# Expert stage of a decoder layer: the down products of six of eight experts taken with the weights stationary and turned back on TensorE

## The chip, the core and the metric

The kernel runs on one core of one Trainium2 chip. The metric is the time of one execution on the device in microseconds (us), the median of several runs. A core has TensorE (PE in the rows, with its weight loads as PEld), VectorE (DVE), ScalarE (ACT), GpSimd (POOL), and a queue of transfers that SyncE issues (SP, SPq).

## What is computed

One decoder layer on 8 sequences of 112 tokens (896 tokens, width D = 512): causal self-attention, a linear cross-attention to a context, and a mixture of eight experts, each followed by a residual add and a layer norm. The change lies in the experts:

```
gate_up = einsum("th,ehj->etj", h, gate_up_proj) + gate_up_bias
gate, up = gate_up[..., ::2], gate_up[..., 1::2]
gate = minimum(gate, 7); up = clip(up, -7, 7)
act = (up + 1) * gate * sigmoid(1.702 * gate)
expert_out = einsum("eti,eih->eth", act, down_proj) + down_proj_bias
out = einsum("te,eth->th", scores, expert_out)      # two experts a token
```

## The kernel before

The program is written by hand, engine by engine; every instruction stands in a fixed queue and waits on counting semaphores. Each float32 matrix is held as a high and a low part (`_hi`, `_lo`), and `products` (L303) makes a product out of three matmuls for each of the KC = 4 chunks of 128 of the contraction, so 12 matmuls for one output bank.

Attention and routing end near 655 us. Routing has by then written each token's row into a table in DRAM (`x_rows`), with room for CAP = 288 rows an expert in a first round; later rounds exist in code and are entered only where an expert has more rows. The 288 rows are handled as PIECES of 128, 128 and 32 rows.

Expert e goes through these steps:

- **Gather.** `gather(e, k)` (L949) turns piece k of the expert's rows with four transposes into a bank (4 or 5 by `gather_bank`, L319); ScalarE (`gathered_high`, L1256) and VectorE (`gathered_low`, L1806) split it into `x_g`.
- **Gate/up.** `gate_up_part(e, q)` (L961), q = 0 to 3, makes 24 matmuls with 128 x 128 weights stationary and the 288 rows moving, into banks q % 2 and 2 + q % 2. Then VectorE clamps (`gl`, `up`), ScalarE takes the sigmoid (`sg`, `swish`), GpSimd multiplies (`pr`, `gated`), VectorE finishes (`hh`, `hidden`), and ScalarE and VectorE split that into `hT` (`h_high` L1269, `h_low`).
- **Down.** `down(e, k)` (L981), k = 0 to 2, has `hT` of a piece stationary (128, 128 and 32 columns) and the 512 columns of `w_dn` moving: 36 matmuls of 512 columns. The result of piece k has its rows on partitions, in bank 6, 7, and 4 or 5 (`y_bank`, L322).
- **Out.** ScalarE scales it by the routing score into `y` (`y_evac`, L1281), and GpSimd adds the rows into `y_acc` in DRAM by an indirect transfer (`add_rows`, L513). The adds of one expert wait until those of the expert before have landed.

TensorE's queue in iteration e (L995 to L1009) is: the four gate/up parts of e, with `gather(e + 1, q - 1)` behind part q = 1, 2 and 3; then the three down pieces of e - 1. The last iteration (e = 7) has no gathers, and `down(7)` follows `down(6)`. ScalarE's queue in iteration e (L1295 to L1320) has, for each q, a cast of the next expert's weights (`gu_high`), the sigmoid of part q, and the `hT` cast of part q - 1; at the end the `hT` cast of part 3, the two first `y_evac` of e - 1, the cast of the next down weights (`dn_high`), and the last `y_evac`. `splits_at` (L314) sets another order of the weight casts for experts 0 and 1: in iteration 1 three of them stand between the `hT` cast of part 3 and the first `y_evac`.

Two semaphores matter most here: `dn_mm` counts finished down pieces, and `y_out` counts `y_evac`. The first gather of an expert waits for the bank that a down result lay in:

```
if k == 0 and e >= 3:
    pe.wait_ge(m["y_out"], 3 * (e - 2))
```

which, for `gather(e + 1, 0)` in iteration e, asks for all three `y_evac` of expert e - 2. SyncE's queue (L424 to L433) loads the down weights of e + 1 once `dn_mm` has reached 3 * e, that is once expert e - 1 is finished with its own.

Of the kernel before, what the change touches and what calls it, by code (L numbers as in the profile page):

```python
# [12 lines left out]
P = 128  # L13
LN_EPS, DEN_EPS = 1e-5, 1e-6
ALPHA, LIMIT = 1.702, 7.0
CAP = 288
# [7 lines left out]
def decoder_layer(nc: bass.Bass, t: dict, out: bass.AP):  # L24
# [20 lines left out]
    with ExitStack() as ctx:  # L45
# [104 lines left out]
        def half_in(hf):  # L150
# [52 lines left out]
        hT = [r(f"hT{s}", 5888 + 2304 * s, (KC, CAP)) for s in range(2)]  # L203
        y = f("y", 24064, 4, D)
        gl = f("gl", 32112, 2, CAP)
        sg = f("sg", 32688, 2, CAP)
# [29 lines left out]
            ones_col sum_mm sum_out bn_ok mv_ok ve_ok rs_ok ln_ok t_hi q2_phi wx_hi wx_lo  # L236
            rz_ok ri_ok a_hi a_lo row_ok id_ok top_ok idx_ok topd_ok topf_ok hot_ok chosen_ok csum_ok dif_ok
            tw_ok prod_ok slotf_ok slot_ok sc_ok score_ok level_ok more_ok gub_ok gate_ok
            gu_hi gu_lo gu_mm gl_ok up_ok sg_ok pr_ok hh_ok h_hi h_lo dn_hi dn_lo dn_mm
            xg_mm xg_hi xg_lo y_out dnb_hi dnb_lo st_hi moreb_ok rest_ok""".split()  # L240
# [81 lines left out]
        def y_bank(e, k):  # L322
            return 6 + k if k < 2 else 4 + (e + 1) % 2
# [141 lines left out]
        def _(pool):  # L465
# [46 lines left out]

            def add_rows(c, number, slot):  # L513
                later = not isinstance(c, int)
                if later or c:
                    pool.wait_ge(add_done, 48 * c)
                    if later:
                        step()
                for k, (p0, rows) in enumerate(PIECES):
# [8 lines left out]
            for e in range(NE + 1):  # L528
                if e < NE:
                    for q in range(KC):  # L530
                        gated(e, q)
                if e == 1:
                    pool.wait_ge(base_out, 16 * (NT + 1))
                    pool.wait_ge(in_meta, 48)
                if e:
                    add_rows(e - 1, lambda k, rows: meta[0:rows, k, e - 1, NE:NE + 1], lambda k: (3 * (e - 1) + k) % 4)
            pool.wait_ge(m["more_ok"], 1)
# [16 lines left out]
        def _(pe):  # L554
# [421 lines left out]
            def down_piece(w, hid, k, bk):  # L976
                p0, rows = PIECES[k]
                products(banks[bk][0:rows, :], lambda a, i: hid[:, a, i, p0:p0 + rows],
                         lambda b, i: w[:, b, i, :], KC).then_inc(m["dn_mm"], 1)

            def down(e, k):  # L981
                if k == 0:
# [49 lines left out]
        def _(act):  # L1032
# [248 lines left out]
            def y_evac(e, k):  # L1281
# [13 lines left out]
            for e in range(NE):  # L1295
                more = e + 1 < NE
                for q in range(KC):
# [21 lines left out]
                if e:  # L1319
                    y_evac(e - 1, 2)  # L1320
            for k in range(3):
                y_evac(NE - 1, k)
            act.wait_ge(m["more_ok"], 1)
# [17 lines left out]
        def _(dve):  # L1341
# [201 lines left out]
            def choose(n):  # L1543
# [4 lines left out]
                dve.wait_ge(*done("rt", n))  # L1548
                nc.vector.max(top[:, s, :], logit[:, s, :]).then_inc(m["top_ok"], 1)
                dve.wait_ge(m["top_ok"], n + 1)  # L1550
                nc.vector.max_index(top_i[:, s, :], top[:, s, :], logit[:, s, :]).then_inc(m["idx_ok"], 1)
# [4 lines left out]
                dve.wait_ge(m["idx_ok"], n + 1)  # L1556
                nc.vector.tensor_copy(top_f[:, s, :], top_i[:, s, 0:2]).then_inc(m["topf_ok"], 1)
                dve.wait_ge(m["topf_ok"], n + 1)
                every = [P, 2, NE]
                nc.vector.tensor_tensor(hot[:, s], iota[:, :].unsqueeze(1).to_broadcast(every),  # L1560
                                        top_f[:, s, :].unsqueeze(2).to_broadcast(every), ALU.is_equal)\
                    .then_inc(m["hot_ok"], 1)
                dve.wait_ge(m["hot_ok"], n + 1)
                nc.vector.tensor_tensor(chosen[:, s, :], hot[:, s, 0], hot[:, s, 1], ALU.add)\
                    .then_inc(m["chosen_ok"], 1)
                nc.vector.tensor_tensor(dif[:, s, :], hot[:, s, 0], hot[:, s, 1], ALU.subtract)\
                    .then_inc(m["dif_ok"], 1)
                dve.wait_ge(m["chosen_ok"], n + 1)
# [4 lines left out]
            def assign(n):  # L1573
# [4 lines left out]
                dve.wait_ge(m["tw_ok"], n + 1)  # L1578
                dve.wait_ge(m["dif_ok"], n + 1)
                nc.vector.scalar_tensor_tensor(sc2[:, s, :], dif[:, s, :], tw[:, s:s + 1], chosen[:, s, :],  # L1580
                                               ALU.mult, ALU.add).then_inc(m["sc_ok"], 1)
                dve.wait_ge(*done("rk", n))
                nc.vector.tensor_tensor(prod[:, s], hot[:, s], pos[:, s, :].unsqueeze(1).to_broadcast([P, 2, NE]),
                                        ALU.mult).then_inc(m["prod_ok"], 1)
                dve.wait_ge(m["sc_ok"], n + 1)
                nc.vector.tensor_scalar(row[:, n, D:D + NE], sc2[:, s, :], 0.5, None, ALU.mult)\
                    .then_inc(m["score_ok"], 1)
                dve.wait_ge(m["prod_ok"], n + 1)
                nc.vector.tensor_reduce(slot_f[:, s, :], prod[:, s], AX.X, ALU.add).then_inc(m["slotf_ok"], 1)
                dve.wait_ge(m["slotf_ok"], n + 1)  # L1590
                nc.vector.tensor_copy(slot_u[:, n, :], slot_f[:, s, :]).then_inc(m["slot_ok"], 1)
# [369 lines left out]
```

## Time and profile before

| | |
|---|---|
| median of 3 runs | 872.35 us (871.97 to 874.51) |
| the profiled execution | 872.94 us, of which the span of the core is 871.1 us |
| TensorE busy | 828.2 us, 95% of the span |
| VectorE, ScalarE, GpSimd busy | 471.7, 310.4, 102.5 us |
| mean granted TensorE clock | 0.973 of full |

A row of the timeline gives start, duration, engine, line, operation, output<-inputs, shapes and count; in brackets stands the idle time before it and what ended that. The start of one group minus that of the one before is the time that the first took up; the durations of neighbours overlap by some 0.1 us. The granted clock (PEclk) is 1.00 at 2.4 GHz and 0.50 at 1.2 GHz.

### The profile page before, as it was taken

To read this page: it belongs to the slowest core of one execution; us is meant where nothing else is said; L and a number is where in the kernel's file an instruction comes from. 1 tells how busy PE (TensorE), PEld (TensorE's weight loads), DVE (VectorE), ACT (ScalarE), POOL (GpSimd) and SP (SyncE) were. 2 spreads that over 40 slices of the span, in tenths; PEclk is the share of its full clock that TensorE was granted. 3 is DMA by queue.
4 is the path that set the end of the run, shared out by engine and by line. 5 is a ranking of instruction groups with operands and counts; after the bars stand their busy time and mean duration, and the time that the engine had idled before them with its cause. 6 is when DMAs were issued, how large, how long until landed. Compare 5 with 4: busy or idle time off the path is not lost.

```text
span 871.1 us, 12501 instructions
## 1 busy us (share of the span) xinstructions
PE 828.2 (95%) x4878; PEld 728.1 (84%) x4878; DVE 471.7 (54%) x862; ACT 310.4 (36%) x700; POOL 102.5 (12%) x95
## 2 busy tenths in 40 slices
PE   7999999999999999999999999999988999999990
PEld 6989898989898898988899878888867888888860
DVE  4536455363635463575760244445686687777624
ACT  4443324242433432442443222221242465555430
POOL 0000000000000000000000000111131244434343
PEclk9999999999999999999999999999976999999995
DMA  9990724523020003003110100110376356656326
GB/s 330 334 295 6 226 109 167 163 81 121 9 94 6 26 6 121 3 4 133 50 36 1 35 6 35 57 61 9 123 284 196 134 190 199 199 173 173 76 34 192
DMA packets 35902, 97.91 MB, mean 112 GB/s; under 512 B 6648, under 2 KB 9080, under 8 KB 33152
## 3 DMA queue, kind: packets, MB, share of 16 engines
q1 hardware_dynamic: 32032, 88.62, 30.0%
q0 software_dynamic: 3808, 8.46, 4.9%
q8 instruction: 40, 0.66, 0.3%
q14 instruction: 22, 0.18, 0.1%
HBM read 64.03 MB, written 32.12 MB: 110 GB/s over the span
## 4 chain that ended last, share of the span: by engine, by line
PE 82%; DVE 7%; DMA 3%; issue 3%; ACT 3%; POOL 1%; POOLq 0%; SPq 0%; DVEq 0%
PE bank L306 66%; PE bank L667 3%; PE bank L701 3%; PE bank L596 3%; PE bank L760 2%; PE bank L655 1%; DVE w_gu L1343 1%; DVE prob L1390 1%; DMA raw_dn<-in_w_down_dram 1%; PE bank L945 1%; PE bank L573 1%; PE bank L739 1%; DMA y_acc<-y,meta 1%; ACT prob L1076 1%; DVE ln_st L1466 1%
## 5 line engine op out<-in xcount | busy, mean ns | idle before, releaser
L306 PE MATMUL bank<-w_kv,cT 128*125 128x512 f32 x576 | 143.6, 400 | 0.0
L306 PE MATMUL bank<-xT,w_qkv 128*128 128x512 f32 (+1 forms) x672 | 137.8, 365 | 0.2 <-ACT qT L1066 0.2
L306 PEld LDWEIGHTS bank<-xT,w_qkv 128*128 128x128 f32 x672 | 122.1, 188 | 15.2 <-ACT qT L1066 0.5
L306 PEld LDWEIGHTS bank<-w_kv,cT 128*125 128x125 f32 x576 | 104.2, 186 | 23.7
L306 PE MATMUL bank<-x_g,w_gu 128*128 128x288 f32 x768 | 111.7, 304 | 3.4 <-DVE x_g L1343 2.9
L306 PEld LDWEIGHTS bank<-x_g,w_gu 128*128 128x128 f32 x768 | 107.5, 195 | 5.1 <-issue 3.2
L475 POOL TENSOR_TENSOR ln_rs<-ln_ve,half 128x1 f32<-128x1 f32 (+2 forms) x16 | 12.7, 792 | 625.6 <-DVE ln_ve L1472 625.5
L306 PE MATMUL bank<-w_o,zT 128*128 128x512 f32 x336 | 79.8, 395 | 0.5 <-DVE acc L1678 0.5
L306 PE MATMUL bank<-w_qkv,xT 128*128 128x256 f32 x588 | 77.3, 287 | 0.0
L306 PEld LDWEIGHTS bank<-w_o,zT 128*128 128x128 f32 x336 | 61.7, 188 | 15.0 <-DVE acc L1377 1.8
L306 PEld LDWEIGHTS bank<-w_qkv,xT 128*128 128x128 f32 x588 | 72.2, 191 | 0.0
L306 PE MATMUL bank<-w_dn,hT 128*128 128x512 f32 (+1 forms) x288 | 68.4, 396 | 0.0
L306 PEld LDWEIGHTS bank<-w_dn,hT 128*128 128x128 f32 (+1 forms) x288 | 45.9, 161 | 19.3
L1343 DVE TENSOR_TENSOR w_qkv<-raw_w,w_qkv 128x1024 fp32r<-128x1024 f32 x21 | 25.7, 1225 | 61.2 <-ACT w_qkv L1034 61.2
L1076 ACT ACTIVATE prob<-prob,neg_max 112x112 f32<-112x112 f32 x128 | 47.7, 374 | 21.9 <-DVE neg_max L1394 21.9
L1103 ACT ACTIVATE relu_c<-bank 125x512 f32<-125x512 f32 x24 | 14.3, 598 | 111.1 <-PE bank L306 111.1
L1086 ACT CAST zT<-bank 128x448 fp32r<-128x448 f32 x32 | 17.0, 533 | 92.5 <-PE bank L667 92.5
L1343 DVE TENSOR_TENSOR w_gu<-raw_gu,w_gu 128x1024 fp32r<-128x1024 f32 x32 | 48.4, 1524 | 0.5 <-ACT w_gu L1034 0.5
L1377 DVE TENSOR_TENSOR acc<-acc,bank 128x512 f32<-128x512 f32 x49 | 33.6, 685 | 24.2 <-PE bank L306 24.2
L523 POOL DMA_INDIRECT y_acc<-y,meta x24 | 39.9, 1662 | 40.8 <-ACT y L1278 34.6
L506 POOL TENSOR_TENSOR pr<-gl,sg 128x288 f32<-128x288 f32 x32 | 32.6, 1019 | 88.3 <-ACT sg L1267 88.3
L1438 DVE SCALAR_TENSOR_TENSOR phi_k<-exp_c,relu_c 125x512 f32<-125x512 f32 x24 | 16.6, 692 | 48.2 <-ACT exp_c L1104 48.2
(150 smaller groups left out, 1155.3 us busy)
## 6 DMA issues: line engine op xcount, KB each, us to landing
x_rows<-blank SPq DMA_DIRECT2D x9, 2084.0 KB, 16.5
raw_gu<-in_w_gu_dram SPq DMA_DIRECT2D x8, 2048.0 KB, 7.8
raw_w<-in_w_qkv_dram SPq DMA_DIRECT2D x22, 512.0 KB, 8.1
raw_dn<-in_w_down_dram SPq DMA_DIRECT2D x8, 1024.0 KB, 9.1
raw_c<-in_ctx_t_dram SPq DMA_DIRECT2D x8, 750.0 KB, 4.3
raw_o<-in_w_o_dram SPq DMA_DIRECT2D x8, 512.0 KB, 4.1
xg<-x_rows SPq DMA_DIRECT2D x8, 512.0 KB, 5.6
raw_kv<-in_w_kv_dram SPq DMA_DIRECT2D x2, 1024.0 KB, 6.8
```

The lines of the kernel that those rows point to most:

```text
L306: last = nc.tensor.matmul(mm_out, lhs(a, k), rhs(b, k), start=(k == 0 and i == 0), stop=(k == n - 1 and i == 2))
L506: nc.gpsimd.tensor_tensor(pr[:, q % 2], gl[:, q % 2], sg[:, q % 2], ALU.mult)\
L523: nc.gpsimd.indirect_dma_start(y_acc, bass.IndirectOffsetOnAxis(ap=number(k, rows).bitcast(U32), axis=0), y[0:rows, slot(k), :], None, bou ...
L596: mm = nc.tensor.matmul(banks[j][:, half_in(hf)], w_first[:, part, a, k, h * E:(h + 1) * E], xT[:, b, k, half_of(hf)], start=(k == 0 and i ...
L667: mm = nc.tensor.matmul(banks[6 + g % 2][:, j * S:(j + 1) * S], V[0:S, p % 2, hf * BH + j, h * E:(h + 1) * E], probT[0:S, g % 2, j, :], st ...
L701: mm = nc.tensor.matmul(banks[4 + g // 2][:, (g % 2) * G1:(g % 2 + 1) * G1], phi_k[0:CM, n % 3, g * P:(g + 1) * P], v_c[0:CM, n % 3, g, :] ...
L760: mm = nc.tensor.matmul(bank("wo", n)[:, :], xT[:, a, k, n * P:(n + 1) * P], w_xo[:, b, k, :], start=(k == 0 and i == 0), stop=(k == KC - ...
L1076: e = nc.scalar.activation(prob[0:S, g, j, :], prob[0:S, g, j, :], ACT.Exp, bias=neg_max[0:S, i:i + 1], scale=-1.0, accum_out=exp_sum[0:S, ...
L1086: nc.scalar.copy(zT[:, 0, h, hf * HALF:(hf + 1) * HALF], banks[6 + g % 2][:, 0:HALF])\
L1343: return nc.vector.tensor_tensor(dst, src, bits(hi), ALU.subtract)
L1377: nc.vector.tensor_tensor(acc[:, n, :], acc[:, n, :], banks[n % 2][:, :], ALU.add)\
L1438: nc.vector.scalar_tensor_tensor(phi_k[0:CM, n % 3, :], exp_c[0:CM, n % 2, :], 1.0, relu_c[0:CM, n % 2, :], ALU.min, ALU.add).then_inc(m[" ...
```

## The change

For experts 0 to 5, `down_turned(e)` takes the place of `down(e, k)`. It has 128 x 128 blocks of `w_dn` stationary and the 288 columns of `hT` moving: four products of 12 matmuls, whose results (128 output columns on partitions, 288 rows along) lie alternately in banks 6 and 7. ScalarE copies each to the new tile `yT` (`y_turned`), and the third product waits for the first copy, the fourth for the second. One iteration later, behind gate/up part 0, `turn_y` turns `yT` back with 12 transposes against `ident` into the banks in which `down` had its results, and `dn_mm` now counts these. ScalarE's `y_evac` of that expert stands behind the sigmoid of part 0 (piece 0) and behind the sigmoid and the `hT` cast that follow part 1 (pieces 1 and 2). GpSimd's adds of expert e - 2 stand one each behind the multiply of parts 1, 2 and 3 of iteration e. Experts 6 and 7 keep `down`, both behind the last gate/up part. Some counters of VectorE's routing steps are merged into two (`pick_ok`, `put_ok`), with the same instructions in the same order.

```diff
+            def down_turned(e):
+                pe.wait_ge(m["dn_lo"], e + 1)
+                pe.wait_ge(m["h_lo"], KC * e + KC)
+                for j in range(KC):
+                    if j >= 2:
+                        pe.wait_ge(m["yt_ok"], KC * e + j - 1)
+                    elif e:
+                        pe.wait_ge(m["y_out"], 3 * (e - 1) + j + 1)
+                    products(banks[6 + j % 2][:, 0:CAP], lambda a, i: w_dn[e % 2][:, a, i, j * P:(j + 1) * P],
+                             lambda b, i: hT[e % 2][:, b, i, :], KC).then_inc(m["dt_mm"], 1)
+
+            def turn_y(e, k):
+                p0, rows = PIECES[k]
+                if k == 0:
+                    pe.wait_ge(m["yt_ok"], KC * e + KC)
+                if k == 2 and e + 2 < NE:
+                    pe.wait_ge(m["xg_lo"], 3 * (e + 2) + 3)
+                for j in range(KC):
+                    mm = nc.tensor.transpose(banks[y_bank(e, k)][0:rows, j * P:(j + 1) * P], yT[:, j, p0:p0 + rows],
+                                             ident[:, :])
+                mm.then_inc(m["dn_mm"], 1)
...
+                    if q == 0 and e >= 2:
+                        for k in range(3):
+                            turn_y(e - 2, k)
                 if e == 0:
                     for k in range(6, 8):
                         pe.wait_ge(free[k], LAST[k])
-                else:
-                    for k in range(3):
-                        down(e - 1, k)
-            for k in range(3):
-                down(NE - 1, k)
+                elif e + 1 < NE:
+                    down_turned(e - 1)
+            for e in (NE - 2, NE - 1):
+                for k in range(3):
+                    down(e, k)
...
+            def y_turned(e):
+                for j in range(KC):
+                    act.wait_ge(m["dt_mm"], KC * e + j + 1)
+                    if j == 0 and e:
+                        act.wait_ge(m["dn_mm"], 3 * e)
+                    nc.scalar.copy(yT[:, j, :], banks[6 + j % 2][:, 0:CAP]).then_inc(m["yt_ok"], 1)
...
+                    if q == 0 and e >= 2:
+                        y_evac(e - 2, 0)
+                    if q == 1 and e >= 2:
+                        y_evac(e - 2, 1)
+                        y_evac(e - 2, 2)
...
-                if e:
-                    y_evac(e - 1, 0)
-                    y_evac(e - 1, 1)
+                if e and more:
+                    y_turned(e - 1)
                 if more:
                     dn_high(e, e % 2)
-                if e:
-                    y_evac(e - 1, 2)
```

How the queues stand before and after, in iteration 5 or 6. Line numbers of the changed file differ by a few (L306, L945, L1273, L1278, L1267, L1034 are now L307, L951, L1304, L1309, L1298, L1065).

TensorE before, from gate/up part 0 of an expert (two runs of 24 `x_g,w_gu` matmuls are parts 0 and 1) to the first gather of the next:

```order
L306 MATMUL bank<-x_g_113,w_gu_101 128x288 [waits up_ok,xg_lo,gu_lo]
L306 MATMUL bank<-x_g_113,w_gu_101 128x288 x23
L306 MATMUL bank<-x_g_113,w_gu_101 128x288 [waits up_ok]
L306 MATMUL bank<-x_g_113,w_gu_101 128x288 x23
L945 MATMUL bank<-ident,xg_110 128x128 [waits y_out,xg_lo,in_xg1]
L945 MATMUL bank<-ident,xg_110 128x128 x3
```

TensorE with the change, from the third product of `down_turned` to the same gather:

```order
L307 MATMUL bank<-hT_115,w_dn_105 128x288 [waits yt_ok]
L307 MATMUL bank<-hT_115,w_dn_105 128x288 x11
L307 MATMUL bank<-hT_115,w_dn_105 128x288 [waits yt_ok]
L307 MATMUL bank<-hT_115,w_dn_105 128x288 x11
L307 MATMUL bank<-x_g_113,w_gu_101 128x288 [waits up_ok,xg_lo,gu_lo]
L307 MATMUL bank<-x_g_113,w_gu_101 128x288 x23
L1005 MATMUL bank<-ident,yT 128x128 [waits yt_ok]
L1005 MATMUL bank<-ident,yT 128x128 x7
...
L307 MATMUL bank<-x_g_113,w_gu_101 128x288 [waits up_ok]
L307 MATMUL bank<-x_g_113,w_gu_101 128x288 x23
L951 MATMUL bank<-ident,xg_110 128x128 [waits y_out,xg_lo,in_xg1]
```

The gather's wait on `y_out` is as it was and asks for the same three `y_evac`; two waits on `yt_ok` are new in the down products.

ScalarE before, from the last gather cast of an iteration through parts 0 and 1 of the next:

```order
L1259 CAST x_g_113<-bank 128x4x32 [waits xg_mm]
L1273 CAST hT_116<-hh 128x288 [waits dn_mm,hh_ok]
L1278 ACTIVATE y<-bank,meta 128x512 [waits dn_mm,add_done] x2
L1034 CAST w_dn_106<-raw_dn_108 128x2048 [waits in_dn1]
L1278 ACTIVATE y<-bank,meta 32x512 [waits dn_mm,add_done]
L1034 CAST w_gu_102<-raw_gu_104 128x1024 [waits in_gu1]
L1267 ACTIVATE sg<-gl 128x288 [waits pr_ok,gl_ok]
L1034 CAST w_gu_102<-raw_gu_104 128x1024 [waits in_gu1]
L1267 ACTIVATE sg<-gl 128x288 [waits pr_ok,gl_ok]
L1273 CAST hT_115<-hh 128x288 [waits dn_mm,hh_ok]
```

ScalarE with the change, the same stretch:

```order
L1304 CAST hT_116<-hh 128x288 [waits dn_mm,hh_ok]
L1326 COPY yT<-bank 128x288 [waits dn_mm,dt_mm]
L1326 COPY yT<-bank 128x288 [waits dt_mm] x3
L1065 CAST w_dn_106<-raw_dn_108 128x2048 [waits in_dn1]
L1065 CAST w_gu_102<-raw_gu_104 128x1024 [waits in_gu1]
L1298 ACTIVATE sg<-gl 128x288 [waits pr_ok,gl_ok]
L1309 ACTIVATE y<-bank,meta 128x512 [waits dn_mm,add_done]
L1065 CAST w_gu_102<-raw_gu_104 128x1024 [waits in_gu1]
L1298 ACTIVATE sg<-gl 128x288 [waits pr_ok,gl_ok]
L1304 CAST hT_115<-hh 128x288 [waits dn_mm,hh_ok]
L1309 ACTIVATE y<-bank,meta 128x512 [waits dn_mm,add_done]
L1309 ACTIVATE y<-bank,meta 32x512 [waits dn_mm,add_done]
```

The four copies of `yT` stand behind the `hT` cast of part 3, and the last two scalings into `y` behind the sigmoid of part 1.

## Rows read from the trace of the kernel before

**Rows 1.** The page, part 1: busy time of each engine.

```profile
PE 828.2 (95%) x4878; PEld 728.1 (84%) x4878; DVE 471.7 (54%) x862; ACT 310.4 (36%) x700; POOL 102.5 (12%) x95
```

**Rows 2.** Timeline of TensorE, iteration of expert 4, in order of time.

```profile
750.00 6.55 PE L306 MATMUL bank<-x_g,w_gu 128*128 128x288 f32 x48
756.39 0.60 PE L945 MATMUL bank<-ident,xg 128*128 128x128 f32 x4
756.75 3.44 PE L306 MATMUL bank<-x_g,w_gu 128*128 128x288 f32 x24
760.03 0.60 PE L945 MATMUL bank<-ident,xg 128*128 128x128 f32 x4
...
764.30 8.59 PE L306 MATMUL bank<-w_dn,hT 128*128 128x512 f32 x36
772.73 6.55 PE L306 MATMUL bank<-x_g,w_gu 128*128 128x288 f32 x48
```

**Rows 3.** Timeline of ScalarE, same iteration: behind part 1, and behind part 3.

```profile
757.94 0.43 ACT L1273 CAST hT<-hh 128x288 fp32r<-128x288 f32 x1 [0.34 <-DVE hh L1836]
758.27 1.05 ACT L1034 CAST w_gu<-raw_gu 128x1024 fp32r<-128x1024 f32 x1
...
768.59 0.43 ACT L1273 CAST hT<-hh 128x288 fp32r<-128x288 f32 x1 [2.00 <-DVE hh L1836]
768.93 0.68 ACT L1278 ACTIVATE y<-bank,meta 128x512 f32<-128x512 f32 x1
```

**Rows 4.** Timeline of ScalarE, end of iteration 1.

```profile
699.80 2.94 ACT L1034 CAST w_gu<-raw_gu 128x1024 fp32r<-128x1024 f32 x3
702.65 1.26 ACT L1278 ACTIVATE y<-bank,meta 128x512 f32<-128x512 f32 x2
```

**Rows 5.** Timeline of TensorE, end of iteration 1 and start of 2.

```profile
695.29 8.61 PE L306 MATMUL bank<-w_dn,hT 128*128 128x512 f32 x36
704.43 6.66 PE L306 MATMUL bank<-x_g,w_gu 128*128 128x288 f32 x48 [0.53 <-DVE w_gu L1343]
```

**Rows 6.** Windows: length, busy time (instructions) by engine, granted clock, DMA share, GB/s.

```profile
660.70:666.60 5.90, 5.86 (x24) 5.89 (x25) 4.49 (x5) 1.44 (x2) 0.00 (x0) 0.50 0.94 316
678.00:679.58 1.58, 0.00 (x0) 0.03 (x1) 1.34 (x4) 0.60 (x2) 0.66 (x1) 1.00 0.83 166
679.58:680.30 0.72, 0.72 (x5) 0.72 (x6) 0.45 (x1) 0.24 (x1) 0.13 (x1) 1.00 0.42 137
680.30:683.70 3.40, 3.40 (x17) 3.40 (x16) 1.33 (x4) 2.43 (x3) 0.00 (x0) 0.50 0.98 419
704.00:706.00 2.00, 1.57 (x12) 1.57 (x13) 0.65 (x2) 2.00 (x2) 1.62 (x1) 1.00 0.55 82
750.00:772.73 22.73, 22.61 (x146) 19.81 (x145) 16.78 (x24) 12.19 (x19) 9.27 (x8) 1.00 0.64 191
```

**Rows 7.** Timeline of TensorE and SyncE's queue, start of iteration 7.

```profile
818.19 12.95 PE L306 MATMUL bank<-x_g,w_gu 128*128 128x288 f32 x96
...
818.39 0.33 SPq L433 DMA_DIRECT2D raw_dn<-in_w_down_dram  x1
```

**Rows 8.** Chain of work that ended last, from iteration 7: start, duration, what.

```profile
818.39 8.50 DMA raw_dn<-in_w_down_dram
826.91 1.91 ACT w_dn L1034
...
841.54 3.77 DMA y_acc<-y,meta
```

**Rows 9.** Timeline of GpSimd, from the multiply of part 3 of iteration 7.

```profile
834.32 0.90 POOL L506 TENSOR_TENSOR pr<-gl,sg 128x288 f32<-128x288 f32 x1 [1.30 <-ACT sg L1267]
837.80 1.58 POOL L523 DMA_INDIRECT y_acc<-y,meta  x1 [2.58 <-ACT y L1278]
...
849.78 1.34 POOL L523 DMA_INDIRECT y_acc<-y,meta  x1 [0.31 <-issue]
```

**Rows 10.** Groups by line and form, 600 to 871: busy us, mean ns of one, idle before.

```profile
L945 PE MATMUL bank<-ident,xg 128*128 128x128 f32 x64 | 10.3, 291 | 2.5 <-DMA xg<-x_rows 2.5
```

More of the change, by code:

```diff
@@ L204, in decoder_layer @@
         y = f("y", 24064, 4, D)
+        yT = f("yT", 30208, KC, CAP)
         gl = f("gl", 32112, 2, CAP)
@@ L511, in step, with add_rows @@
                 pool.drain()
-            def add_rows(c, number, slot):
+            def add_rows(c, number, slot, which=(0, 1, 2)):
                 later = not isinstance(c, int)
-                if later or c:
+                if (later or c) and which[0] == 0:
                     pool.wait_ge(add_done, 48 * c)
@@ L518, in add_rows @@
                         step()
-                for k, (p0, rows) in enumerate(PIECES):
+                for k in which:
+                    p0, rows = PIECES[k]
                     pool.wait_ge(m["y_out"], 3 * c + k + 1)
@@ L526, in add_rows, with add_tiled @@
                         .then_inc(add_done, 16)
[L528 to L534, printed above, removed]
-                if e:
-                    add_rows(e - 1, lambda k, rows: meta[0:rows, k, e - 1, NE:NE + 1], lambda k: (3 * (e - 1) + k) % 4)
+            def add_tiled(e, which):
+                add_rows(e, lambda k, rows: meta[0:rows, k, e, NE:NE + 1], lambda k: (3 * e + k) % 4, which)
+            for e in range(NE):
+                for q in range(KC):
+                    gated(e, q)
+                    if e == 2 and q == 1:
+                        pool.wait_ge(base_out, 16 * (NT + 1))
+                        pool.wait_ge(in_meta, 48)
+                    if q and e >= 2:
+                        add_tiled(e - 2, (q - 1,))
+            for e in (NE - 2, NE - 1):
+                add_tiled(e, (0, 1, 2))
             pool.wait_ge(m["more_ok"], 1)
@@ L979, in down_piece @@
                          lambda b, i: w[:, b, i, :], KC).then_inc(m["dn_mm"], 1)
+            def down_turned(e):
[9 more added lines that the diff above has]
+            def turn_y(e, k):
+                p0, rows = PIECES[k]
+                if k == 0:
[6 more added lines that the diff above has]
+                mm.then_inc(m["dn_mm"], 1)
             def down(e, k):
@@ L1006, in _ @@
                         pe.wait_ge(free[k], LAST[k])
-                else:
-                    for k in range(3):
-                        down(e - 1, k)
-            for k in range(3):
-                down(NE - 1, k)
+                elif e + 1 < NE:
+                    down_turned(e - 1)
+            for e in (NE - 2, NE - 1):
+                for k in range(3):
+                    down(e, k)
             pe.wait_ge(m["more_ok"], 1)
@@ L1313, in _ @@
                     gu_high(e + 1, (e + 1) % 2, k)
-                if e:
-                    y_evac(e - 1, 0)
-                    y_evac(e - 1, 1)
+                if e and more:
+                    y_turned(e - 1)
                 if more:
                     dn_high(e, e % 2)
-                if e:
-                    y_evac(e - 1, 2)
-            for k in range(3):
-                y_evac(NE - 1, k)
+            for e in (NE - 2, NE - 1):
+                for k in range(3):
+                    y_evac(e, k)
             act.wait_ge(m["more_ok"], 1)
@@ L1548, in choose @@
                 dve.wait_ge(*done("rt", n))
-                nc.vector.max(top[:, s, :], logit[:, s, :]).then_inc(m["top_ok"], 1)
-                dve.wait_ge(m["top_ok"], n + 1)
-                nc.vector.max_index(top_i[:, s, :], top[:, s, :], logit[:, s, :]).then_inc(m["idx_ok"], 1)
+                nc.vector.max(top[:, s, :], logit[:, s, :]).then_inc(m["pick_ok"], 1)
+                dve.wait_ge(m["pick_ok"], 5 * n + 1)
+                nc.vector.max_index(top_i[:, s, :], top[:, s, :], logit[:, s, :]).then_inc(m["pick_ok"], 1)
                 if n >= 2:
@@ L1555, in choose @@
                     .then_inc(m["topd_ok"], 1)
[L1556 to L1558 removed]
+                dve.wait_ge(m["pick_ok"], 5 * n + 2)
+                nc.vector.tensor_copy(top_f[:, s, :], top_i[:, s, 0:2]).then_inc(m["pick_ok"], 1)
+                dve.wait_ge(m["pick_ok"], 5 * n + 3)
                 every = [P, 2, NE]
@@ L1578, in assign @@
                 dve.wait_ge(m["tw_ok"], n + 1)
-                dve.wait_ge(m["dif_ok"], n + 1)
+                dve.wait_ge(m["pick_ok"], 5 * n + 5)
                 nc.vector.scalar_tensor_tensor(sc2[:, s, :], dif[:, s, :], tw[:, s:s + 1], chosen[:, s, :],
-                                               ALU.mult, ALU.add).then_inc(m["sc_ok"], 1)
+                                               ALU.mult, ALU.add).then_inc(m["put_ok"], 1)
                 dve.wait_ge(*done("rk", n))
                 nc.vector.tensor_tensor(prod[:, s], hot[:, s], pos[:, s, :].unsqueeze(1).to_broadcast([P, 2, NE]),
-                                        ALU.mult).then_inc(m["prod_ok"], 1)
-                dve.wait_ge(m["sc_ok"], n + 1)
+                                        ALU.mult).then_inc(m["put_ok"], 1)
+                dve.wait_ge(m["put_ok"], 3 * n + 1)
                 nc.vector.tensor_scalar(row[:, n, D:D + NE], sc2[:, s, :], 0.5, None, ALU.mult)\
                     .then_inc(m["score_ok"], 1)
-                dve.wait_ge(m["prod_ok"], n + 1)
-                nc.vector.tensor_reduce(slot_f[:, s, :], prod[:, s], AX.X, ALU.add).then_inc(m["slotf_ok"], 1)
-                dve.wait_ge(m["slotf_ok"], n + 1)
+                dve.wait_ge(m["put_ok"], 3 * n + 2)
+                nc.vector.tensor_reduce(slot_f[:, s, :], prod[:, s], AX.X, ALU.add).then_inc(m["put_ok"], 1)
+                dve.wait_ge(m["put_ok"], 3 * n + 3)
                 nc.vector.tensor_copy(slot_u[:, n, :], slot_f[:, s, :]).then_inc(m["slot_ok"], 1)
```

12 lines of the change are left out of this document (6 added, 6 removed).

## The prediction

> **What bounds the kernel now.** I read the busy times first: TensorE is busy 828.2 of 871.1 us [rows 1], so TensorE's queue is the bound and the other engines count only where TensorE waits for them. The windows confirm it for the changed stage: in the iteration of expert 4, from 750.00 to 772.73, TensorE is busy 22.61 of 22.73 us at a clock of 1.00, VectorE 16.78 and ScalarE 12.19 [rows 6]. Next I read TensorE's timeline for that iteration [rows 2], since starts of neighbouring groups give real costs: 48 gate/up matmuls with 288 columns moving take 756.39 - 750.00 = 6.39 us, four transposes take 756.75 - 756.39 = 0.36, the 36 down matmuls take 772.73 - 764.30 = 8.43. Then ScalarE's timeline [rows 3, 4], because the change hangs TensorE on ScalarE in two places; last the end of the program [rows 7 to 9], which is a chain of transfers and adds and no longer TensorE alone. The sum is made against the profiled execution, 872.94 us; the median of the runs is 0.6 lower. About 0.3%, 2.6 us, is what a measurement of this kernel can tell from no change.
>
> **TensorE's work.** Per turned expert the change removes 36 matmuls of 512 columns, 8.43 us, and adds 48 of 288 columns. The same shape with the same count stands in the gate/up parts: 6.39 us [rows 2]. It adds 12 transposes; I take those of the gather, 0.36 us for four, so 1.08 [rows 2]. Net 8.43 - 6.39 - 1.08 = **0.96 us less**, times six 5.8. That is the whole gain, if nothing waits.
>
> The Trainium skill, TensorE: Matmul & The Clock Gate, section "Part 4: PE-mode transpose", puts a 128x128 transpose at about 275 ns in a kernel's context, and with it the turn-back would cost an estimated 3.3 us an expert. The gather rows say 90 ns for the same form, and the measurement decides.
>
> **New wait 1: the gather.** `gather(e + 1, 0)` stands right behind gate/up part 1 and needs all three `y_evac` of e - 2. Before, these were a whole iteration old. Now the last two stand on ScalarE behind the sigmoid of part 1 and the `hT` cast behind it, so they cannot begin before part 1 has ended and gone through VectorE and ScalarE. The trace shows this path already: part 1 ends at 756.39 [rows 2], that `hT` cast runs at 757.94 and ScalarE is free for the next instruction at 758.27 [rows 3]. Two scalings into `y` take 1.26 us [rows 4], so the gather may start at 759.53, **3.14 us late**. It happens in iterations 2 to 6, five times. Behind it in the queue stand parts 2 and 3, the other gathers and the next down products, and nothing can pass.
>
> **New wait 2: the third down product.** Products 0 and 1 need 24 x 288-column matmuls, 3.20 us (half of 6.39). Product 2 needs copy 0 out of bank 6, and that copy stands on ScalarE behind the `hT` cast of part 3. The down stretch begins at 764.30 [rows 2]; ScalarE begins its first instruction behind that cast at 768.93 [rows 3], the copy is of the cast's size, 0.43, say 0.45 with its signal: 769.38, against 767.50 when TensorE gets there: **1.88 us late**. The `hT` cast is that late since VectorE has a weight split and gather splits ahead of the last `hh`; none of that moves. Product 3 finds its copy done. This happens in iterations 2 to 6, five times. In iteration 1 three weight casts stand between: ScalarE is free at 702.65 [rows 4], the copy ends at 703.10, and TensorE, which began the down stretch at 695.29 [rows 5], waits from 698.49, **4.61 us**. Gate/up of expert 2 then begins at 703.10 + 3.20 = 706.30 in place of 704.43: 1.87 us later in all.
>
> **Sum for the iterations.** For 2 to 6: 22.73 - 8.43 + 6.39 + 1.08 + 3.14 + 1.88 = 26.79, which is 4.06 more; times five 20.3. With iteration 1: **22.2 us**.
>
> **What I cost at nothing.** ScalarE gets four copies of 0.45 us, 1.8 on 12.19 busy of 22.73 [rows 6]. The cast of the down weights now stands behind the last copy, so VectorE's low part of them ends a little into the next iteration and delays the clamps of part 0 by about a microsecond; part 2 needs those only 4 us later. SyncE loads the next down weights after the turn-back, 4.4 us into the next iteration in place of its start; the transfer takes 8.5 us [rows 8] and its cast is wanted at the end of that iteration, 20 us in. Row loads queued behind it are wanted an iteration later. GpSimd's adds go between its multiplies, 1.6 us each in gaps of 3 us. The merged counters have the same instructions in the same order on one engine.
>
> **The end.** In iteration 7 this cover is gone. The load of expert 7's down weights is issued 0.20 us after the start of gate/up [rows 7], and its cast holds up ScalarE's queue at part 1 [rows 8]. Now it is issued behind gate/up part 0 (3.28 us, rows 2: 756.75 to 760.03) and the turn-back (1.08): 4.36 us later, and the multiply of part 3, at 834.32 - 818.19 = 16.13 us into the iteration [rows 9], comes at 20.49. On GpSimd the last add of expert 5 now stands behind it: 0.90 for the multiply, then 3.77 until the add has landed [rows 8], 25.16. Only then may the adds of expert 6 start, which began at 837.80 - 818.19 = 19.61 [rows 9]: **5.6 us later**. From there to the last add it is 12.0 us as before, on the same chain of adds.
>
> Waits and work together: 22.2 + 5.6 = **27.8 us**.
>
> **The clock.** The only comparable wait in the stage shows what a pause does. TensorE idles from 678.00 to 679.58, goes on at 1.00 for 0.72 us, is granted 0.50 (1.2 GHz) from 680.30 to 683.70 and has 1.00 (2.4 GHz) in the windows from 704.00 on [rows 6]. In those 3.40 us it does half the work: 1.70 us lost. The pause of 0.53 us before 704.43 [rows 5] cost nothing, the clock stayed at 1.00 [rows 6]. All eleven new pauses (five of 3.14, five of 1.88, one of 4.61) are longer than the one of 1.58. Their price is bounded below by nothing (the fall might not come every time) and above by the stretch from 660.70 to 666.60, 5.90 us at 0.50 after a pause that came on top of little work [rows 6], 2.95 us. I take the nearest row, 1.70: 11 x 1.70 = **18.7 us**. Nothing hides it, since it falls on TensorE's own work.
>
> The forecast is 872.94 + 27.8 + 18.7 = 919.4, less 0.6 to the median: **919 us**.
>
> **Rivals.**
>
> 1. *The clock stays up.* One fall is little evidence, and between the new pauses TensorE always has at least 3 us of dense work. If none came: 872.35 + 27.8 = 900 us. Against it: the shorter pause did bring one. If only the six long ones did, 910. I give the whole of "no fall" 0.07; the part case belongs to the forecast.
>
> 2. *Falls or turns cost more than taken.* With 2.95 us a pause: 872.35 + 27.8 + 32.5 = 933 us. A mechanism of the same size is the turn-back itself, if its transposes, whose stationary operand ScalarE has just written, do not stream as the gather's do: at the gather transposes' own duration, 291 ns from start to end [rows 10], twelve take 3.5 us in place of 1.08, and 919 + 6 x 2.4 = 933. Against both: these transposes have the gather's form, and in this iteration four of them cost 0.36 us [rows 2]. Chance 0.06 for the clock, 0.03 for the transposes. The page's 275 ns stands for the same case and would give 932 by its estimate.
>
> 3. *Faster: the results are out in time.* ScalarE has 10.5 us free in an iteration, and TensorE is the bound; if `y_evac` of e - 2 and copy 0 came before TensorE asks, only the 0.96 us an expert would be left: 872.35 - 5.8 = 867 us, if the later load at the end were hidden too. The place is the first gather of iterations 2 to 6, and it decides by whether that gather starts less than 0.96 us after part 1 has ended. Against it: the scalings stand behind a sigmoid that part 1 itself feeds; 1.9 us pass in rows 2 and 3 before ScalarE is free even without them. 0.03.
>
> 4. *The waits are half as long*, because work that a late TensorE lets the others finish shortens the chains: about 872.35 + 5.6 + 1.9 + 5 x 1.5 + 11 x 0.85 = 897 us. Against it: both chains start at the end of a gate/up part, so lateness elsewhere does not shorten them. 0.04.
>
> **How the numbers follow.** Forecast 0.77, rivals 0.07, 0.09, 0.03, 0.04. The range runs from 902, a little above no falls, to 931, a little below the dear cases; at most 2 in 10 lie outside. Faster by over 0.3%: 0.03. Within 0.3%: 0.02, room for rival 3 if the end stays as late. Slower: 0.95.
>
> **What would show it.** In the changed profile: TensorE's first gather of iterations 2 to 6 with some 3.1 us idle before it, ended by ACT `y`; the 288-column down matmuls with 1.9 us idle in their middle, ended by ACT `yT`, 4.6 in the first expert; 12 transposes in 1.1 us; starts of gate/up 26.8 us apart plus up to 3.4 for the clock; 0.50 in windows behind each pause; the load of the last down weights 4.4 us into iteration 7. I would be wrong if the gather started at once, if the clock were 1.00 in windows behind the pauses, or if iterations were shorter than 22.7 us.

## The result, and the profile after

The changed kernel takes 906.27 us (902.9 to 908.92, 4 runs) against 873.43 us (4 runs) of the kernel before: a ratio of 1.037, 95% interval 1.034 to 1.041, so 3.7% slower. The forecast was 919 with a range of 902 to 931. The profiled execution took 902.9 us, 30.0 more than the one of before. Below, a fall means that the granted clock went from 1.00 to 0.50 for some microseconds, and gate/up 2 means the gate/up parts of expert 2.

TensorE's timeline in the iteration of expert 3, which answers to [rows 2]: start, duration, work, and in brackets the idle time before it with what ended it.

```profile
733.68 3.36 PE L307 MATMUL bank<-x_g,w_gu 128*128 128x288 f32 x24
736.88 1.47 PE L1005 MATMUL bank<-ident,yT 128*128 128x128 f32 x12
738.11 3.44 PE L307 MATMUL bank<-x_g,w_gu 128*128 128x288 f32 x24
744.65 0.63 PE L951 MATMUL bank<-ident,xg 128*128 128x128 f32 x4 [3.10 <-ACT y L1309]
745.04 3.43 PE L307 MATMUL bank<-x_g,w_gu 128*128 128x288 f32 x24
...
752.58 3.46 PE L307 MATMUL bank<-hT,w_dn 128*128 128x288 f32 x24
757.65 3.46 PE L307 MATMUL bank<-hT,w_dn 128*128 128x288 f32 x24 [1.61 <-ACT yT L1326]
760.95 3.36 PE L307 MATMUL bank<-x_g,w_gu 128*128 128x288 f32 x24
```

Both pauses are where the forecast put them, ended by the instructions it named. The iteration takes 760.95 - 733.68 = 27.27 us in place of 22.73, and the same 27.27 in each of the five. The waits of TensorE over the whole stage (total, times, longest):

```profile
PE bank L951 <- ACT y L1309: 15.5, 5, 3.1
PE bank L307 <- ACT yT L1326: 12.4, 6, 4.3
```

ScalarE's timeline at the two places answers to [rows 3]:

```profile
742.14 0.44 ACT L1298 ACTIVATE sg<-gl 128x288 f32<-128x288 f32 x1 [1.30 <-DVE gl L1864]
742.93 0.43 ACT L1304 CAST hT<-hh 128x288 fp32r<-128x288 f32 x1 [0.34 <-DVE hh L1877]
743.26 1.24 ACT L1309 ACTIVATE y<-bank,meta 128x512 f32<-128x512 f32 x2
...
756.87 0.43 ACT L1304 CAST hT<-hh 128x288 fp32r<-128x288 f32 x1 [2.00 <-DVE hh L1877]
757.21 0.69 ACT L1326 COPY yT<-bank 128x288 f32<-128x288 f32 x2
```

The scalings end at 743.26 + 1.24 = 744.50, and the gather starts at 744.65. The first copy starts at 757.21, and the third down product at 757.65.

TensorE's timeline in iteration 1, the windows there (length, busy by engine, clock, DMA share, GB/s) and those behind three of the 3.1 us pauses, beside [rows 5, 6]:

```profile
693.24 3.46 PE L307 MATMUL bank<-hT,w_dn 128*128 128x288 f32 x24
701.02 5.55 PE L307 MATMUL bank<-hT,w_dn 128*128 128x288 f32 x24 [4.32 <-ACT yT L1326]
706.41 3.36 PE L307 MATMUL bank<-x_g,w_gu 128*128 128x288 f32 x24
```

```profile
701.00:705.00 4.00, 3.98 (x16) 3.98 (x17) 1.31 (x2) 0.67 (x2) 0.00 (x0) 0.50 0.00 0
744.00:748.00 4.00, 3.35 (x26) 3.38 (x27) 0.99 (x2) 1.44 (x2) 2.08 (x1) 1.00 0.38 38
771.00:775.00 4.00, 3.08 (x24) 3.11 (x25) 1.26 (x2) 1.71 (x3) 2.35 (x1) 1.00 0.39 55
799.00:803.00 4.00, 3.80 (x30) 3.83 (x31) 0.54 (x2) 0.99 (x2) 1.64 (x1) 1.00 0.49 55
```

Here the forecast missed: of the eleven pauses only the one of 4.32 us brought the clock to 0.50 (24 matmuls then took 5.55 us in place of 3.46). Behind the others it stayed at 1.00.

The end, beside [rows 7 to 9]: TensorE's and SyncE's start of iteration 7, ScalarE's cast, and GpSimd.

```profile
842.77 3.36 PE L307 MATMUL bank<-x_g,w_gu 128*128 128x288 f32 x24
...
847.48 0.33 SPq L434 DMA_DIRECT2D raw_dn<-in_w_down_dram  x1
...
853.51 1.89 ACT L1065 CAST w_dn<-raw_dn 128x2048 fp32r<-128x2048 f32 x1
...
862.38 1.40 POOL L525 DMA_INDIRECT y_acc<-y,meta  x1 [0.17 <-issue]
866.25 1.56 POOL L525 DMA_INDIRECT y_acc<-y,meta  x1 [2.47 <-ACT y L1309]
...
879.28 1.33 POOL L525 DMA_INDIRECT y_acc<-y,meta  x1 [0.30 <-issue]
```

The last add starts 879.28 - 842.77 = 36.51 us after gate/up 7 began, against 849.78 - 818.19 = 31.59 before. The load of the down weights is issued 4.71 us into the iteration, but its cast has no idle time before it: it did not wait for the load.

The 30.0 us in one line: iteration 1 from its down products to gate/up 2 takes 13.17 in place of 9.14 (+4.0, of which 2.1 are the clock), the iterations 2 to 6 take 136.4 in place of 113.8 (+22.6), the end +4.9, the stretch behind the last add +0.5; against that the start of the down products in iteration 1 came 2.05 us earlier (693.24 against 695.29). Half of that is there at gate/up 1 already (678.55 against 679.58). The other half is the clock, which after the pause of 1.77 us stayed up this time: parts 0 and 1 took up 6.48 us in place of 8.00, and 0.5 of that went into longer waits behind them.

### The profile page after: what moved, and what is told of

Read it like the earlier page. It is cut to its first block and busy times, and to the rows that moved or that the text cites. A ratio compares the mean times of both kernels' runs of the same rounds, so it can differ in the third digit from the quotient of the medians.

```text
span 901.1 us, 12818 instructions
## 1 busy us (share of the span) xinstructions
PE 826.8 (92%) x5022; PEld 739.3 (82%) x5022; DVE 471.6 (52%) x862; ACT 317.5 (35%) x724; POOL 111.5 (12%) x95
## 5 line engine op out<-in xcount | busy, mean ns | idle before, releaser
L307 PE MATMUL bank<-w_kv,cT 128*125 128x512 f32 x576 | 143.5, 400 | 0.0
L307 PE MATMUL bank<-xT,w_qkv 128*128 128x512 f32 (+1 forms) x672 | 137.8, 365 | 0.2 <-ACT qT L1097 0.2
L307 PEld LDWEIGHTS bank<-xT,w_qkv 128*128 128x128 f32 x672 | 122.1, 188 | 15.2 <-ACT qT L1097 0.5
L307 PEld LDWEIGHTS bank<-w_kv,cT 128*125 128x125 f32 x576 | 104.2, 186 | 23.7
L307 PE MATMUL bank<-x_g,w_gu 128*128 128x288 f32 x768 | 110.8, 301 | 3.1 <-DVE x_g L1384 2.9
L307 PEld LDWEIGHTS bank<-x_g,w_gu 128*128 128x128 f32 x768 | 105.3, 191 | 3.8 <-issue 3.2
L476 POOL TENSOR_TENSOR ln_rs<-ln_ve,half 128x1 f32<-128x1 f32 (+2 forms) x16 | 12.7, 794 | 625.3 <-DVE ln_ve L1513 625.2
L307 PE MATMUL bank<-w_o,zT 128*128 128x512 f32 x336 | 79.8, 395 | 0.5 <-DVE acc L1719 0.5
L307 PE MATMUL bank<-w_qkv,xT 128*128 128x256 f32 x588 | 77.3, 287 | 0.0
L307 PEld LDWEIGHTS bank<-w_o,zT 128*128 128x128 f32 x336 | 61.7, 188 | 15.0 <-DVE acc L1418 1.9
L307 PEld LDWEIGHTS bank<-w_qkv,xT 128*128 128x128 f32 x588 | 72.2, 191 | 0.0
L307 PE MATMUL bank<-hT,w_dn 128*128 128x288 f32 x288 | 43.6, 309 | 12.4 <-ACT yT L1326 12.4
L307 PEld LDWEIGHTS bank<-hT,w_dn 128*128 128x128 f32 x288 | 40.8, 197 | 14.1 <-ACT yT L1326 13.8
L525 POOL DMA_INDIRECT y_acc<-y,meta x24 | 48.0, 2001 | 10.9 <-ACT y L1309 6.7
```

Source lines behind the costliest of these rows:

```text
L307: last = nc.tensor.matmul(mm_out, lhs(a, k), rhs(b, k), start=(k == 0 and i == 0), stop=(k == n - 1 and i == 2))
L476: nc.gpsimd.tensor_tensor(ln_rs[:, ln, n0:n1], ln_ve[:, ln, n0:n1], half[:, n0:n1], ALU.pow)\
L525: nc.gpsimd.indirect_dma_start(y_acc, bass.IndirectOffsetOnAxis(ap=number(k, rows).bitcast(U32), axis=0), y[0:rows, slot(k), :], None, bou ...
```

## The experiments

Two theories went in. Mine: two orders on ScalarE make TensorE wait, some 23 us, and a late end adds 5. The rivals: the waits are coupled, so that taking one away moves it to another place, or the clock is the larger part. Medians below stand beside 873.65 us of before for the first four runs and 874.09 for the next three.

**One: the scalings earlier.**

```diff
-                        y_evac(e - 2, 0)
-                    if q == 1 and e >= 2:
-                        y_evac(e - 2, 1)
-                        y_evac(e - 2, 2)
+                        for k in range(3):
+                            y_evac(e - 2, k)
```

> The changed kernel with the second and third scaling into y moved on ScalarE from behind part 1 to behind the sigmoid of part 0, beside the first. Theory 1 (the gather of iterations 2 to 6 waits for exactly these two scalings): TensorE's idle before the first gather, 3.1 us five times, goes to nothing, iterations shrink from 27.27 to about 24.0 us, and the median falls from 906 by 16 to 19 us (the upper end if fewer clock falls come with it), to 887 to 890. The waits of 1.6 us in the down products stay. Rival (the lateness sits in TensorE's queue as a whole, and another wait takes over): the idle reappears in the down products or at gate/up part 2, and the median stays above 900.

Measured: 885.09 us, 21.2 less than the changed kernel. TensorE's waits on `y` are gone, those on `yT` are as they were:

```profile
PE bank L307 <- ACT yT L1326: 12.4, 6, 4.3
```

Iterations take 23.97 us, 3.30 less, times five 16.5. The last add comes 34.6 us after gate/up 7 in place of 36.5, for ScalarE is through with the scalings before part 1. So the gather's wait costs what it lasts and does not move elsewhere. The median fell by 2 us more than the upper end expected. The iterations and the end make 18.4 of the 21.2; the profiled executions differ by 19.5. The rest was not traced; the changed kernel's median lies 3.4 above its own profiled execution, with lower mean clocks (0.962 to 0.966 against 0.969), so clock falls are the likely part.

**Two: the copies earlier.**

```diff
+                if e and more:
+                    y_turned(e - 1, (0, 1))
                 h_high(e, KC - 1, hT[e % 2])
+                if e and more:
+                    y_turned(e - 1, (2, 3))
                 for k in splits_at(e, KC):
                     gu_high(e + 1, (e + 1) % 2, k)
-                if e and more:
-                    y_turned(e - 1)
```

> The changed kernel with the first two copies into yT moved on ScalarE ahead of the hT cast of part 3 (and in iteration 1 ahead of three weight casts). Theory 1 (the third down product waits for ScalarE's order, not for the copy itself): the idle in the middle of the down products, 1.6 us five times and 4.3 once, goes to nothing, iterations shrink by 1.8 us, and the median falls from 906 by 13 to 17 us to 889 to 893. The gather's wait of 3.1 us stays. Rival (TensorE only gets earlier to the gather, which waits for a chain that starts elsewhere): the gather's wait grows by what the other loses, and the median stays within 3 us of 906.

Measured: 901.06 us, 5.2 less than the changed kernel and not 13 to 17. TensorE's timeline shows both reasons:

```profile
705.05 5.39 PE L307 MATMUL bank<-x_g,w_gu 128*128 128x288 f32 x24 [4.96 <-DVE w_gu L1386]
...
770.42 0.72 PE L951 MATMUL bank<-ident,xg 128*128 128x128 f32 x4 [3.11 <-ACT y L1309]
770.80 4.97 PE L307 MATMUL bank<-x_g,w_gu 128*128 128x288 f32 x24
...
779.88 6.65 PE L307 MATMUL bank<-hT,w_dn 128*128 128x288 f32 x48
786.37 3.36 PE L307 MATMUL bank<-x_g,w_gu 128*128 128x288 f32 x24
```

The wait within the down products is gone: 48 matmuls run through in 6.49 us (779.88 to 786.37). But in iteration 1 my edit put copies 2 and 3, which wait for TensorE, ahead of the three weight casts, and gate/up 2 now waits 4.96 us for those weights: what was gained there is lost. And the gather's pause, with its length unchanged, now brought the clock down four times of five:

```profile
768.00:772.00 4.00, 1.58 (x9) 1.61 (x10) 2.76 (x4) 2.86 (x5) 3.26 (x2) 0.85 0.44 170
772.00:776.00 4.00, 4.00 (x26) 4.00 (x24) 0.19 (x1) 0.00 (x0) 0.00 (x0) 0.72 0.50 66
```

Part 2 takes 4.97 us in place of 3.44 behind it. The rival's prediction, a gather wait that grows, did not come: it stays at 3.11.

**Three: both.** The two edits together.

> Both moves together. Theory 1: no wait of TensorE over 0.5 us is left in iterations 2 to 6, iterations take 22.73 - 8.43 + 6.60 + 1.23 = 22.1 us, the clock never falls there, and only the later end of some 5 us stands against the gain of 0.6 us an expert: 871 to 875, the same as before within 0.3%. Rival (the clock is the larger cost, or the two waits are coupled): above 880.

Measured: 876.63 us (10 runs), ratio to before 1.003, interval 1.001 to 1.005. That is 1.6 above the expected range. Iterations 3 to 6 take 22.1 us as worked out, and the clock is up in them; the waits do not couple. The 4.96 us before gate/up 2, made by my own edit, and the late end hold the total above before:

```profile
PE bank L307 <- DVE w_gu L1384: 5.0, 1, 5.0
```

**Four: the load of the down weights earlier.**

```diff
-                    sp.wait_ge(m["dn_mm"], 3 * e)
+                    sp.wait_ge(m["dt_mm"], KC * e)
```

> The changed kernel with the load of the next down weights issued when the four turned products are done, not when they are turned back. Theory 1 (the later end of 4.9 us comes from that load and what its cast holds up): the load is issued at the start of iteration 7 again, the sigmoid of part 2 comes some 2 us after part 1 has ended or later by the cast alone, and the median falls from 906 by 3 to 5 us to 901 to 903. Rival (the end is late because the last add of expert 5 now stands behind the last multiply on GpSimd): at most 1.5 us.

Measured: 902.73 us, 3.5 less than the changed kernel, by the median just what my theory said. The trace says otherwise. The load is issued 0.2 us into iteration 7 (842.70, gate/up begins at 842.50), and nothing that follows has moved:

```profile
853.24 1.89 ACT L1065 CAST w_dn<-raw_dn 128x2048 fp32r<-128x2048 f32 x1
```

That is 10.74 us after the start of gate/up 7, as in the changed kernel (853.51 - 842.77). The last add is at 36.28 in place of 36.51. The theory of the load is out. The medians differ by how high the clock was: one of the four runs took 908.33 us at a mean clock of 0.962, the three others 902.0 to 902.9 at 0.969 or 0.970, and the changed kernel's four stand the same way, from 902.9 at 0.969 to 908.92 at 0.962.

**Five: the adds earlier.** Each of GpSimd's adds stands one multiply earlier.

```diff
-                    if e == 2 and q == 1:
+                    if e == 2 and q == 0:
                         pool.wait_ge(base_out, 16 * (NT + 1))
                         pool.wait_ge(in_meta, 48)
-                    if q and e >= 2:
-                        add_tiled(e - 2, (q - 1,))
+                    if q < 3 and e >= 2:
+                        add_tiled(e - 2, (q,))
```

> The changed kernel with only GpSimd's adds each one multiply earlier (add k of expert e - 2 behind the multiply of part k). Theory 1, new (the early load having done nothing: the end of iteration 7 is late since the add of expert 5's last piece stands behind the last multiply, and the adds of expert 6 wait until it has landed): the first add of expert 6 comes at 21.2 us after the start of gate/up 7 in place of 23.5, the last add 2.2 us earlier than now, 34.3; the median 2 us lower, 902 to 905, with 1 to 8 us of clock falls besides. Rival (the scaling of expert 6 behind the last hT cast sets it): first add not before 23 us, no difference.

Measured: 904.11 us. GpSimd's timeline, with gate/up 7 beginning at 846.10:

```profile
863.09 1.39 POOL L525 DMA_INDIRECT y_acc<-y,meta  x1 [0.16 <-issue]
864.24 1.08 POOL L507 TENSOR_TENSOR pr<-gl,sg 128x288 f32<-128x288 f32 x1
867.90 1.59 POOL L525 DMA_INDIRECT y_acc<-y,meta  x1 [2.58 <-ACT y L1309]
...
880.38 1.34 POOL L525 DMA_INDIRECT y_acc<-y,meta  x1 [0.30 <-issue]
```

The first add of expert 6 comes at 21.80 in place of 23.48, the last at 34.28 in place of 36.51: 2.2 us of the 4.9 are this order. Against before 2.7 are left. 2.0 of them are there already at the multiply of part 3 (18.14 against 16.13). It stands behind the last cast of the down weights, which starts 10.74 us into the iteration in place of 8.72 (826.91 - 818.19). Run one shows 1.1 of these 2.0 to be the two scalings ahead of that cast: with them moved, the cast starts at 9.59 and the multiply comes at 17.02. The turn-back, 1.23 us of TensorE's queue ahead of part 1, is likely the rest; no run takes it away.

**Six: everything, and the weight casts spread.** The edits of runs one, two, four and five; in iteration 1 the weight casts are spread over the parts, and the last stands ahead of copies 2 and 3:

```diff
-        SPLITS = {0: ((3,), (), (), (), ()), 1: ((), (), (), (0,), (1, 2, 3))}
+        SPLITS = {0: ((3,), (), (), (), ()), 1: ((), (0,), (1,), (2,), (3,))}
```

> The changed kernel with both ScalarE moves, the load of the down weights when the products are done, each of GpSimd's adds one multiply earlier, and the weight casts of iteration 1 spread over its parts (the 4.96 us before gate/up 2 in the run of both moves had three casts behind the last copies). Theory 1: TensorE has no wait over 0.5 us from expert 2 on, gate/up 2 follows its down products at once (against the run of both moves 5 us less, and 1.5 more without the clock fall behind that wait), iterations stay at 22.1, the last add comes 32 to 34 us after the start of gate/up 7: 867 to 870 us, faster than before by 0.4 to 0.8%. Rival (the product change is worth nothing, since some other engine limits the iteration once TensorE does not): iterations of 22.7 us and 872 to 875.

Measured: 867.39 us (6 runs, 866.6 to 868.1), ratio 0.992, interval 0.991 to 0.994: faster than before. One iteration on TensorE:

```profile
722.16 3.36 PE L307 MATMUL bank<-x_g,w_gu 128*128 128x288 f32 x24
725.36 1.47 PE L1005 MATMUL bank<-ident,yT 128*128 128x128 f32 x12
726.59 3.44 PE L307 MATMUL bank<-x_g,w_gu 128*128 128x288 f32 x24
...
737.77 6.66 PE L307 MATMUL bank<-hT,w_dn 128*128 128x288 f32 x48
744.27 0.96 PE L307 MATMUL bank<-x_g,w_gu 128*128 128x288 f32 x6
```

22.11 us an iteration, no wait over 0.33 us from gate/up 2 on, the clock at 1.00 from 699 to 815 us. The last add comes at 32.88 (843.45 - 810.57): with scalings and adds both moved, 3.6 of the 4.9 us at the end are gone. The down stretch is 6.50 + 1.23 = 7.73 us against 8.43 [rows 2]: the swap of the operands is worth 0.6 to 0.7 us an expert, if nothing waits for it.

**Seven: the kernel before with the casts spread**, the line `SPLITS` alone.

> The kernel before, with only the weight casts of iteration 1 spread over its parts as in the run of everything early. This tells what of that run's gain is not the products'. Theory 1: it removes the pause of 0.53 us before gate/up 2 and nothing else, at most 0.6 us: 873 to 874. Rival (the casts crowd VectorE in iteration 1): 0.5 to 2 us slower.

Measured: 872.68 us (12 runs), ratio 0.998, interval 0.997 to 1.000: at most 0.3%. Run six is 5.3 us faster than this one, so its gain is not the casts'. It is not all the products' either. Between the two profiled executions (5.1 us), the stretch from the down products of iteration 1 to gate/up 7 gives 4.6, the products' share; 2.0 were gained ahead of these products, where both kernels have the same work, by a clock that rose earlier and did not fall behind the pause of 1.77 us; the end costs 1.4.

**Eight: the changed kernel three times more**, to count the clock falls.

> The changed kernel as it is, once more, to count clock falls behind the same eleven pauses. Theory (the waits are the same in every execution, the falls are not): gather waits of 3.1 us five times, product waits of 1.6 five times and 4.3 once, as before; the number of 288-column groups of 24 that take 4.6 us or more in place of 3.4 differs between executions, from 1 to 5, each worth 1.5 to 2.1 us, and the span follows that number: about 901 with one, 907 with four or five. Rival (the first forecast's: a pause of this length always brings a fall): eleven, and a span near 918.

For the other two the text on record was:

> As the first repetition: the same waits, 1 to 5 falls, the span 901 to 907 with their number; the rival has eleven falls.

> As the first repetition: the same waits, 1 to 5 falls, the span 901 to 907 with their number; the rival has eleven falls.

The spans were 902.4, 906.0 and 899.6 us. The waits are the same to 0.1 us in all. The slow groups of the second, behind the pause of 1.77 us in iteration 1 and behind 4.33 and two of 3.1:

```profile
680.20 8.14 PE L307 MATMUL bank<-x_g,w_gu 128*128 128x288 f32 x48 [1.77 <-DVE x_g L1384]
703.68 4.98 PE L307 MATMUL bank<-hT,w_dn 128*128 128x288 f32 x24 [4.33 <-ACT yT L1326]
802.03 5.61 PE L307 MATMUL bank<-x_g,w_gu 128*128 128x288 f32 x24
831.83 4.51 PE L307 MATMUL bank<-x_g,w_gu 128*128 128x288 f32 x24
```

Its siblings have two such groups (behind 1.77 and 4.33) and one (behind 4.33). Over the four profiled executions of the changed kernel, the profile after among them:

| pause before it | falls |
|---|---|
| 1.6 us, product 2 | 0 of 20 |
| 1.77 us, start of iteration 1, as before the change | 2 of 4 |
| 3.1 us, gather | 2 of 20 |
| 4.3 us, product 2 of the first expert | 4 of 4 |

Runs four and five have the same waits on TensorE; in their two profiles the pauses of 3.1 us brought one fall of ten, those of 1.6 none, the two of 4.3 one each, and those of 1.77 none.

So the rival of this run, the first forecast's rule, is out. The falls are most of the spread between executions: at the start of gate/up 7 the second repetition is 7.3 us behind the third, 5.0 of them by its three more falls (1.0, 2.5 and 1.4), 1.0 by a clock that rose later in gate/up 0, and 1.3 from ahead of the experts.

For the pause of 1.77 us the profiles show what goes with a fall, though no run shows it to be the cause. Ahead of it, the first gate/up group of expert 0 (24 matmuls) starts at 0.50 in every profile, and the clock rises towards its end. In the five profiles in which that group lasted 5.84 us or more (before, runs three and seven, the first two repetitions) the pause brought a fall; in the seven in which it lasted 5.44 or less (the profile after, runs one, two, four, five and six, the third repetition) it brought none. So with equal pauses the outcome went with the moment at which the clock had risen before.

## Why the prediction was right or wrong

- **What bounds**: right. TensorE's queue set the iterations, and ScalarE counted only at the two waits.
- **TensorE's work**: forecast 0.96 us less an expert, measured 8.43 - 6.50 - 1.23 = 0.70 where nothing waits (run six). The 12 transposes took 1.23 us in place of 1.08, the 48 matmuls 6.50 in place of 6.39. The page's 275 ns for a transpose (the Trainium skill, TensorE: Matmul & The Clock Gate, "Part 4: PE-mode transpose") did not hold for these rows as a price; one costs 1.23 / 12 = 0.10 us in the queue, though each lasts 272 ns from start to end, close to that figure (four of the twelve turn only 32 rows, and last as long).
- **Wait 1, the gather**: forecast 3.14 us five times; the trace has 3.1 idle. Between the end of part 1's slot (738.11 + 3.28) and the gather lie 3.26 us. Run one confirms it by taking it away.
- **Wait 2, the third product**: forecast 1.88 and 4.61, measured 1.6 and 4.3 idle; with what TensorE needs to stop and start, 1.77 (757.65 - 752.58 less 3.30). Runs two and three confirm it.
- **Iterations**: forecast 26.79, measured 27.27. The 0.48 us are small errors of the terms: the down matmuls take 6.60 around the pause in place of 6.39 (+0.21), the transposes +0.15, the gather's wait +0.12, parts 0 and 1 without their pause 6.48 in place of 6.39 (+0.09), a gather +0.03, the second wait -0.11.
- **The end**: forecast 5.6 us later, measured 4.9, but the step "it is issued 4.36 us later, and the multiply of part 3 comes at 20.49" was wrong. I carried the load's delay through, as if its cast still waited for it, and took the load's 8.5 us from before. The load took 4.8 us this time and was there. The multiply came at 18.15. Run four takes the load out as a cause, run five shows the order of the adds for 2.2 us; the rest is mostly the 2.0 us by which the multiply of part 3 comes later, at least 1.1 of them from the scalings (run one). The 12.0 us "as before" from the first add of expert 6 to the last add were 13.0 (879.28 - 866.25), so two errors cancel: 3.9 us later at that first add in place of 5.6, and 1.0 more behind it. That the sum came within 0.7 us is partly luck.
- **The clock**: the step that failed is "11 x 1.70 = 18.7 us". The price of a fall was about right (1.4 to 2.5 us where one came behind a new pause), the number was not: 1 to 3 of the eleven new pauses brought one in the four profiled executions, some 1.5 to 5.5 us in all. The prediction's own sign of being wrong, a clock of 1.00 in windows behind the pauses, came at eight to ten of the eleven. I generalised from one pause of 1.58 to 1.77 us, and this one, at the same place, has itself brought a fall in only two of four executions. The clock term is some 13 to 17 us too large; the forecast lies only 12.7 us over the median since the iterations and the median of before were each a little dearer than taken. The time lies within the range because its lower end was set just above no falls, not because the forecast of the clock held.
- **Rivals**: the end on the faster side needed the results in time. Run six is this case, built: with the waits gone 867.39, near the 867 that the rival gave. That the figures agree so closely is partly chance: the products gave 4.6 us and not 5.8, the end cost 1.4, and the clock ahead of them gave 2.0. "The clock stays up" gave 900, and the fastest repetition took 901.4, so this rival, with a chance of 0.07, came nearer than the forecast. Dear transposes (3.5 us) and waits of half the length did not come: 1.23 us, and 3.1 and 1.6.

## What to carry to other kernels

A shorter product is worth its difference only if its results are out of the banks when the next user of the bank comes up in the queue: before moving an evacuation, look what stands ahead of it on its engine, and whether that is fed by the very work the reader stands behind. Here 0.7 us an expert was bought with 5 us of waits, and moving a few instructions turned 3.7% slower into 0.8% faster. A delay is carried along a chain only through links that were waiting: where slack exists, subtract it before adding the delay on, and don't take a median that agrees for the mechanism (run four).

## What the runs showed of the hardware

A pause of TensorE does not have a fixed price. One of 4.3 us brought the granted clock to 0.50 every time; one of 3.1 us did so 2 times of 20 in the changed kernel and 4 of 5 in run two, though part 1 stood directly in front of it and the gather and part 2 behind it in both. What differed is that run two has no pause in the down products, and so another length of iteration (25.4 us without a fall and 26.9 with one, against 27.27). The pause of 1.77 us brought a fall in five of twelve profiles, and these are the five in which the clock had risen latest in the work of expert 0 before it. So the outcome does not hang on the length of a pause alone. Why is open: a run that shifts the same pause step by step was not tried. Where a fall came, 24 matmuls of 288 columns took 4.5 to 5.6 us in place of 3.4.

The last load of 1 MB of down weights took 8.5 us before and 4.8 in the changed kernel. The moment of its issue is not the reason: run four issues it 0.20 us into iteration 7, as before, and it takes 4.8. What differs is the company: in its 8.50 us before, the transfers moved 188 GB/s, some 1.6 MB, so 0.6 MB of others ran beside it; in its 4.80 us in run four they moved 218 GB/s, 1.05 MB, the load alone. Which of the others slowed it was not tried.
